# Output maps in fifteen even pieces, two features in every place, Gelu ahead of the map piece, and the weights' steps later in a turn

## The chip, the cores and the metric

The kernel runs on one core of one Trainium2 chip. The metric is the device time of one execution in microseconds (us). Three executions of the kernel before took 2920.89, 2920.94 and 2922.76 us, so its median is 2920.94 us.

## What is computed

The reference has two layers with a residual sum each. The first is a state-space layer: a kernel K of 2048 taps for each of 512 features, made from 64 complex modes, is convolved with the normalised input (8 rows of 2048 steps), Gelu follows, and the result is normalised and added. The second is a recurrent layer with gates f, i and g over 128 steps, of which only the last cell state is used, and an output product.

```
x = x + layernorm(gelu(conv(layernorm(x), K) + D * layernorm(x)))
for t in steps:
    c = sigmoid(xt @ wf.T + c @ uf.T + bf) * c + sigmoid(xt @ wi.T + c @ ui.T + bi) * tanh(xt @ wc.T + c @ uc.T + bc)
h = tanh(x @ wo.T + c_final @ uo.T + bo)
x = x + layernorm(h)
```

The shapes as the harness cuts them: x is 8 x 2048 x 512; the second layer goes over the first dimension, 8 steps of 2048 rows, so its eight blocks of 256 rows each run 8 steps.

## The kernel before

The work has three stages. A prologue (to about 141 us of the span) takes row statistics, makes K and the powers of the state matrix, and starts on the first group of features. The convolution stage (141.74 to 637 us) is where the change lies. The last stage, from there to the end, is the recurrent layer; the change does not touch it.

**The convolution stage.** The 512 features are cut into 16 groups of 32. The sequence is cut into 16 chunks of 128 steps. Within a chunk the convolution is a Toeplitz product (`conv_input`, float32, tiles `T` and `u`). Across chunks it goes through a state of 128 numbers: 15 states per group, each made from the one before (`state_in`, `state_high`, `state_low`), and an output map per feature, 128 x 128, applied to the states (`conv_state`, three float16 products per feature). The output map of a group is made by doubling: step k = -1 and 0 give single columns, step k doubles the number of columns from 2^k, and the last, k = 6, makes columns 64 to 127 (`outm`). Steps are cut into pieces by features, because a bank takes 512 columns: `PIECES` lists (k, first feature, last feature). There are 12 pieces in the kernel before, whose widths are 32, 32, 64, 128, 256 columns and then seven times 512.

A **turn** i (1 to 16) convolves group i-1 while it makes the states and the maps of group i. It has 16 **places** j. In place j stand state 15i+j (j below 15), piece j of the map (where there is one), the features that `CONV_AT[j]` names, and the weights' steps of that place. TensorE, ScalarE, VectorE and the queue of SyncE each run through the places in this order; every engine executes its own list strictly in the order in which it is written, and waits on semaphores.

- On TensorE a place is: `state_high(j)`, the two or so `conv_input`, `state_low(j)`, `state_in(j+1)`, the `conv_state`, then `outm(j)`, then `turn` or `spread` of the weights.
- State j goes from the bank through ScalarE (`state`, high half, L737) and VectorE (`state`, low half, L1001). `state_high(j+1)` waits for the first, `state_low(j+1)` (L1304) for the second.
- A map piece goes the same way: ScalarE L748, then VectorE L1011. The next step of the doubling waits for VectorE's part of the whole step before.
- A Gelu (L801) takes four features at once, so it stands in the places where the fourth feature of a bank is done.

**The weights.** In turns 1 to 15 the eight weight matrices of the second layer are split into float16 parts. A matrix set n goes through in turn n (n = 0 and 1 both in turn 1). For n mod 4 of 0 or 1 there are four maxima (`most`, VectorE L1069); for 1 there follow `most2` (VectorE L1071), `turn` (a transpose on TensorE, L1386), `most3` (VectorE L1074, L1075), `spread` (TensorE L1389) and `most4` (VectorE L1079 to L1082), which give the scale. For n mod 4 of 2 or 3 there are four `cut` (ScalarE L820) and four `cut2` (VectorE L1086), and then a store to `wd`. The places in which they stand are in `weight_steps`. Below, a turn with `cut` is a **cut turn** (2, 3, 6, 7, 10, 11, 14, 15) and one with `most` a **most turn** (1, 4, 5, 8, 9, 12, 13); of these 1, 5, 9 and 13 also have the five steps from `most2` to `most4`.

**Other engines.** GpSimd normalises `u` of group i+1 in turn i, with two instructions of 1024 columns for each of four quarters (L619, L621). The SyncE queue issues, at the start of turn i: four loads of `u` (which wait until the convolution of turn i-1 is done), the load of the weights `wts`, a load of `T` from `kpad`, the store of `y` of group i-2; later the second `T`, and in a cut turn the store of `wd` after `cut2` number 3. A DMA that has to wait for its semaphore holds everything behind it in this queue.

Of the kernel before, what the change touches and what calls it, by code (L numbers as in the profile page):

```python
# [16 lines left out]
G = 32  # L17
NG = H // G
# [62 lines left out]

def piece_done(g, k):

    return NP * g + max(i for i, p in enumerate(PIECES) if p[0] == k) + 1


def weight_steps(i):

    at = {j: [] for j in range(-1, 16)}

    def steps(n, places):
        if n % 4 < 2:
            names = [("load", 0)] + [("most", f) for f in range(4)]
            if n % 4:
                names += [("most2", 0), ("turn", 0), ("most3", 0), ("spread", 0), ("most4", 0)]
        else:
            names = [("load", 0)] + [("cut", f) for f in range(4)] + [("cut2", f) for f in range(4)]
        for j, (name, f) in zip(places, names):
            at[j].append((name, n, f))
# [6 lines left out]
    return at  # L106
# [49 lines left out]
def s4_lstm_program(nc, x, xr, xg, wts, cst, small, four, out):  # L156
    ctx = ExitStack()
    with ctx:
# [13 lines left out]
        s = {n: ctx.enter_context(nc.semaphore(f"s_{n}")) for n in names}  # L172
# [166 lines left out]
        def sync_program(e):  # L339
            w = Engine(e)  # L340
# [58 lines left out]
            for i in range(1, NG + 1):  # L399
                tasks = weight_steps(i)  # L400

                def weights(j):
                    for step, n, f in tasks[j]:
# [88 lines left out]
            for j in range(8):  # L492
                for b in range(8):
                    i = 8 * j + b
# [205 lines left out]
        def act_program(e):  # L700
# [38 lines left out]
            def outm(g, i):  # L739
                k, h0, h1 = PIECES[i]  # L740
                n = NP * g + i
# [61 lines left out]
            for i in range(1, NG + 1):  # L803
                tasks = weight_steps(i)
                for j in range(16):
                    if i < NG and j < 15:
                        state(15 * i + j)
                    if i < NG and j < NP:
                        outm(i, j)
                    for h in CONV_AT[j]:  # L810
                        conv(i - 1, h)
                    for step, n, f in tasks[j]:
# [69 lines left out]
        def dve_program(e):  # L882
# [120 lines left out]
            def outm(g, i):  # L1003
                k, h0, h1 = PIECES[i]
                n = NP * g + i
# [49 lines left out]
            for i in range(1, NG + 1):  # L1055
                tasks = weight_steps(i)
                for j in range(16):
# [4 lines left out]
                    for step, n, f in tasks[j]:  # L1062
# [145 lines left out]
        def pe_program(e):  # L1208
# [97 lines left out]
            def outm(g, i):  # L1306
                k, h0, h1 = PIECES[i]
                n = NP * g + i
# [27 lines left out]
            def conv_state(g, h):  # L1336
# [3 lines left out]
                w.wait_ge(s["omlo"], NP * g + NP)  # L1340
# [51 lines left out]
            for i in range(1, NG + 1):  # L1392
                tasks = weight_steps(i)
                for j in range(16):
# [14 lines left out]
                    for step, n, f in tasks[j]:  # L1409
                        weights(step, n)  # L1410
# [154 lines left out]
```

## Time and profile before

| | us |
|---|---|
| median of 3 runs | 2920.94 |
| the profiled execution, its own time | 2926.07 |
| its span, first to last instruction | 2924.3 |
| mean granted TensorE clock | 0.983 of full speed |
| TensorE busy / weight load busy | 2791.8 (95%) / 2285.4 (78%) |
| VectorE / ScalarE / GpSimd busy | 1664.1 (57%) / 994.7 (34%) / 790.0 (27%) |

All trace rows come from the profiled execution, which took 5.13 us longer than the median of the runs. 1.77 us of its time lie outside the span. Busy shares are means over three unlike stages; what the change can do has to be read in the convolution stage, turn by turn. A turn is counted here from the first `conv_input` of its place 0 to the first of the next turn. By that count turns 1 to 16 start at 141.74, 179.10, 210.77, 242.42, 276.11, 307.92, 339.47, 371.39, 402.71, 436.53, 468.19, 499.86, 531.27, 562.74, 594.25 and 623.59 us.

### The profile page before, as it was taken

To read this page: it belongs to the slowest core of one execution; us is meant where nothing else is said; L and a number is where in the kernel's file an instruction comes from. 1 tells how busy PE (TensorE), PEld (TensorE's weight loads), DVE (VectorE), ACT (ScalarE), POOL (GpSimd) and SP (SyncE) were. 2 spreads that over 40 slices of the span, in tenths; PEclk is the share of its full clock that TensorE was granted. 3 is DMA by queue.
4 is the path that set the end of the run, shared out by engine and by line. 5 is a ranking of instruction groups with operands and counts; after the bars stand their busy time and mean duration, and the time that the engine had idled before them with its cause. 6 is when DMAs were issued, how large, how long until landed. Compare 5 with 4: busy or idle time off the path is not lost.

```text
span 2924.3 us, 57067 instructions
## 1 busy us (share of the span) xinstructions
PE 2791.8 (95%) x23628; PEld 2285.4 (78%) x23628; DVE 1664.1 (57%) x3615; ACT 994.7 (34%) x1982; POOL 790.0 (27%) x1187
## 2 busy tenths in 40 slices
PE   3589999999999999999999999999999999999998
PEld 2377777778887788778877887788788878877884
DVE  7854545556456555665466556655655566456535
ACT  6655545542223322332223223222332232232223
POOL 7776656611112111221122112211221122112102
PEclk7799999999999999999999999999999999999999
DMA  8867768783222222222321322221322233222201
GB/s 322 282 226 256 244 219 279 251 288 94 48 46 61 66 64 50 65 63 60 71 66 45 81 43 70 69 59 37 80 65 52 44 77 69 47 52 71 66 14 58
DMA packets 404549, 308.65 MB, mean 106 GB/s; under 512 B 274368, under 2 KB 340416, under 8 KB 398016
## 3 DMA queue, kind: packets, MB, share of 16 engines
q1 hardware_dynamic: 404288, 305.00, 37.1%
q8 instruction: 185, 3.03, 0.4%
q14 instruction: 76, 0.62, 0.1%
HBM read 195.88 MB, written 76.02 MB: 93 GB/s over the span
## 4 chain that ended last, share of the span: by engine, by line
PE 86%; DVE 6%; DMA 4%; ACT 2%; issue 1%; SPq 1%; POOL 0%; DVEq 0%; POOLq 0%; ACTq 0%
PE bank L1433 34%; PE bank L1444 30%; PE bank L1472 10%; DMA big<-wts 3%; PE bank L1334 2%; PE bank L1284 2%; PE bank L1342 2%; PE bank L1320 2%; PE bank L1459 1%; DVE big L1086 1%; DVE big L1020 1%; PE bank L1296 1%; PE bank L1304 1%; DVE big L1011 1%; ACT big L748 1%
## 5 line engine op out<-in xcount | busy, mean ns | idle before, releaser
L1433 PE MATMUL bank<-big 128*128 128x256 f16 x9216 | 1038.7, 273 | 2.7 <-DVE big L1129 1.5
L1433 PEld LDWEIGHTS bank<-big 128*128 128x128 f16 x9216 | 902.4, 98 | 126.3 <-DVE big L1129 1.8
L1444 PE MATMUL bank<-big 128*128 128x256 f16 x8064 | 911.2, 273 | 0.0
L1444 PEld LDWEIGHTS bank<-big 128*128 128x128 f16 x8064 | 789.0, 98 | 95.8
L852 ACT ACTIVATE big<-bank,big 128x256 f32<-128x256 f32 x768 | 402.5, 561 | 1145.5 <-PE bank L1444 1128.6
L1158 DVE TENSOR_TENSOR big<-big 128x256 f32<-128x256 f32 x224 | 94.8, 423 | 574.2 <-ACT big L852 571.8
L1472 PE MATMUL bank<-big 128*128 128x512 f16 x1536 | 348.8, 379 | 0.0
L1472 PEld LDWEIGHTS bank<-big 128*128 128x128 f16 x1536 | 150.3, 98 | 160.3
L661 POOL TENSOR_SCALAR big<-big 128x1 f32<-128x1 f32 x128 | 33.0, 258 | 795.7 <-DVE big L1110 794.3
L676 POOL TENSOR_SCALAR big<-big 128x1 f32<-128x1 f32 x128 | 28.5, 223 | 796.3 <-DVE big L1189 796.3
L859 ACT ACTIVATE big<-big 128x512 f32<-128x512 f32 x128 | 80.6, 630 | 465.2 <-DVE big L1185 465.2
L1160 DVE TENSOR_TENSOR big<-big 128x256 f32<-128x256 f32 x256 | 108.9, 426 | 170.9 <-ACT big L852 164.6
L619 POOL TENSOR_TENSOR big<-big 128x1024 f32<-128x1024 f32 x63 | 150.8, 2394 | 155.5 <-DMA big<-xg 155.3
L1001 DVE SCALAR_TENSOR_TENSOR big<-bank,big 128x256 f16<-128x256 f32 x240 | 101.2, 422 | 122.7 <-ACT big L737 122.3
L1334 PE MATMUL bank<-big 128*128 128x128 f32 x1024 | 157.6, 279 | 1.5 <-POOL big L630 1.5
L621 POOL TENSOR_TENSOR big<-big 128x1024 f32<-128x1024 f32 x63 | 155.3, 2465 | 4.9
L1011 DVE SCALAR_TENSOR_TENSOR big<-bank,big 128x32 f16<-128x32 f32 (+2 forms) x192 | 101.7, 530 | 94.8 <-ACT big L748 94.3
L1284 PE MATMUL bank<-big 128*128 128x256 f32 x480 | 146.5, 388 | 6.4 <-DVE big L993 6.4
L1334 PEld LDWEIGHTS bank<-big 128*128 128x128 f32 x1024 | 134.4, 193 | 4.4 <-issue 1.9
L748 ACT ACTIVATE big<-bank 128x32 f16<-128x32 f32 (+2 forms) x192 | 91.1, 474 | 132.2 <-PE bank L1320 132.1
L1192 DVE TENSOR_TENSOR big<-big 128x512 f32<-128x512 f32 x128 | 88.7, 693 | 67.9 <-ACT big L866 67.1
L1342 PEld LDWEIGHTS bank<-big 128*128 128x128 f16 x1536 | 103.1, 98 | 30.9 <-issue 0.5
(188 smaller groups left out, 2865.2 us busy)
## 6 DMA issues: line engine op xcount, KB each, us to landing
big<-xr SPq DMA_DIRECT2D x16, 2048.0 KB, 11.1
big<-xg SPq DMA_DIRECT2D x64, 512.0 KB, 6.3
big<-kpad SPq DMA_DIRECT2D x32, 1024.0 KB, 11.7
yd<-big SPq DMA_DIRECT2D x16, 2048.0 KB, 17.3
big<-x SPq DMA_DIRECT2D x64, 512.0 KB, 6.0
out<-big SPq DMA_DIRECT2D x128, 256.0 KB, 2.1
big<-yd SPq DMA_DIRECT2D x62, 512.0 KB, 6.7
big<-wts SPq DMA_DIRECT2D x16, 1024.0 KB, 9.8
```

Source lines behind the costliest of these rows:

```text
L619: e.tensor_tensor(ug, ug, st(0), SUB).then_inc(s["sub"], 1)
L621: e.tensor_tensor(ug, ug, st(1), MUL).then_inc(s["nrm"], 1)
L748: e.activation(M[g % 2][:, 0, h0:h1, lo:lo + wide], o, ACT.Copy, scale=BACK).then_inc(s["omhi"], 1)
L852: e.activation(gt[m % 2][:, g, :], gate_out(m, g), ACT.Tanh if g == 2 else ACT.Sigmoid, bias=bs, scale=inv[g]).then_inc(s["ga"], 1)
L1011: e.scalar_tensor_tensor(Mg[:, 1, h0:h1, lo:lo + wide], o, BACK, Mg[:, 0, h0:h1, lo:lo + wide], MUL, SUB).then_inc(s["omlo"], 1)
L1160: ch().tensor_tensor(gb[:, 1, :], gb[:, 1, :], gb[:, 2, :], MUL).then_inc(s["c"], 1)
L1284: ins = e.matmul(o, Gm, u[g % 3][:, k].rearrange("p h b -> p (h b)"), start=True, stop=(k == 0))
L1334: e.matmul(o, T[t % 3][:, h % 16, :], u[g % 3][:, :, h, :], start=(q == 0), stop=False, skip_group_check=True)
L1342: ins = e.matmul(o[:, 1:16], M[g % 2][:, lw, h, :], X[g % 2][:, :, lx, h, :], start=False, stop=(a == 2), skip_group_check=True)
L1433: ins = e.matmul(gate_out(m, g), W[2 * g][:, lw, kt, m * 128:(m + 1) * 128], src[:, lx, kt, :], start=(n == 0 and g != 1), stop=last, skip ...
L1444: ins = e.matmul(gate_out(m, g), W[2 * g + 1][:, lw, kt, m * 128:(m + 1) * 128], src[:, lx, kt, :], start=False, stop=(n == 11), skip_grou ...
L1472: ins = e.matmul(bH[n % NH][:, :], x2T[i % R][:, lx, kt, cc * 128:(cc + 1) * 128], W[6][:, lw, kt, :], start=(a == 0), stop=(a == 11))
```

## The change

Four things change in the convolution stage, all of them in the order and the size of the work; no sum over columns changes.

1. **The maps.** Groups 1 to 15 get 15 pieces: the first six as before (32, 32, 64, 128, 256, 512 columns), step 5 in pieces of 12, 12 and 8 features (384, 384, 256 columns), step 6 in pieces of 6, 6, 5, 5, 5, 5 features (384, 384, 320, 320, 320, 320 columns). Group 0, made in the prologue, keeps the 12 pieces. `piece_base` counts the pieces for both.
2. **The features.** `CONVS` was 2 in places 0 to 10, 0 in place 11, 2 in 12 to 14 and 4 in 15; now it is 2 in each of the 16 places. Since a Gelu takes four features, it now stands in every odd place.
3. **ScalarE's order.** In a place the Gelu now stands ahead of the map piece.
4. **The weights' places.** `most` moves from places 4, 6, 8, 10 to 7, 8, 9, 10; `most2` and `turn` from 11 and 12 to 11 both; `most3` and `spread` from 13 and 14 to 12 both; `most4` from 15 to 13. `cut` moves from 5, 7, 9, 11 to 10, 11, 12, 13 and `cut2` from 6, 8, 10, 12 to 12, 13, 14, 15. In turn 1 the four `most` of n = 0 move from places 2, 2, 3, 3 to 7, 7, 8, 8; the load of n = 1 from place 4 to 8 and its `most` from 8, 8, 9, 9 to 14, 14, 15, 15; its five further steps from places 11 to 15 of turn 1 to places 0, 0, 1, 1, 2 of turn 2.

```diff
-PIECES = [(-1, 0, G)] + [(k, 0, G) for k in range(5)] + [(5, 0, 16), (5, 16, 32)] + [(6, 8 * i, 8 * i + 8) for i in range(4)]
+PIECES_0 = [(-1, 0, G)] + [(k, 0, G) for k in range(5)] + [(5, 0, 16), (5, 16, 32)] + [(6, 8 * i, 8 * i + 8) for i in range(4)]
+PIECES = PIECES_0[:6] + [(5, a, b) for a, b in ((0, 12), (12, 24), (24, 32))] + [(6, a, b) for a, b in ((0, 6), (6, 12), (12, 17), (17, 22), (22, 27), (27, 32))]
-CONVS = [2] * 11 + [0] + [2] * 3 + [4]
+CONVS = [2] * 16
...
+def piece_base(g):
+
+    return len(PIECES_0) + NP * (g - 1) if g else 0
...
-    if i == 1:
-        steps(0, (-1, 2, 2, 3, 3))
-        steps(1, (4, 8, 8, 9, 9, 11, 12, 13, 14, 15))
-    elif i < 16:
-        steps(i, (-1, 4, 6, 8, 10, 11, 12, 13, 14, 15) if i % 4 < 2 else (-1, 5, 7, 9, 11, 6, 8, 10, 12))
+        if n == 0:
+            at[1, -1].append(("load", n, 0))
+            places = [("most", f, 1, 7 + f // 2) for f in range(4)]
+        elif n == 1:
+            at[1, 8].append(("load", n, 0))
+            places = [("most", f, 1, 14 + f // 2) for f in range(4)]
+            places += [("most2", 0, 2, 0), ("turn", 0, 2, 0), ("most3", 0, 2, 1), ("spread", 0, 2, 1), ("most4", 0, 2, 2)]
         else:
+            at[n, -1].append(("load", n, 0))
+            if n % 4 < 2:
+                places = [("most", f, n, 7 + f) for f in range(4)]
+                if n % 4:
+                    places += [("most2", 0, n, 11), ("turn", 0, n, 11), ("most3", 0, n, 12), ("spread", 0, n, 12), ("most4", 0, n, 13)]
+            else:
+                places = [("cut", f, n, 10 + f) for f in range(4)] + [("cut2", f, n, 12 + f) for f in range(4)]
...
                 for j in range(16):
                     if i < NG and j < 15:
                         state(15 * i + j)
+                    for h in CONV_AT[j]:
+                        conv(i - 1, h)
                     if i < NG and j < NP:
                         outm(i, j)
-                    for h in CONV_AT[j]:
-                        conv(i - 1, h)
...
-                w.wait_ge(s["omlo"], NP * g + NP)
+                w.wait_ge(s["omlo"], piece_base(g + 1))
```

**Where the order moves.** TensorE in places 11 to 14 of turn 5. Before (L1320 is a map piece, L1296 and L1304 are `state_high` and `state_low`, L1334 `conv_input`, L1284 `state_in`, L1342 `conv_state`, L1386 `turn`, L1389 `spread`):

```order
L1320 MATMUL bank<-big 128x512 x3
L1296 MATMUL bank<-big 128x256 x2
L1334 MATMUL bank<-big 128x128 x2
L1304 MATMUL bank<-big 128x256
L1284 MATMUL bank<-big 128x256
L1342 MATMUL bank<-big 128x120 x6
L1386 MATMUL bank<-big 1x128
L1296 MATMUL bank<-big 128x256 x2
...
L1342 MATMUL bank<-big 128x120 x6
L1389 MATMUL bank<-big 128x1
```

The same engine and places now (L1332 is the map piece, L1398 `turn`, L1401 `spread`, L1308 and L1316 the state, L1346 `conv_input`, L1296 `state_in`, L1354 `conv_state`):

```order
L1354 MATMUL bank<-big 128x120 x6
L1332 MATMUL bank<-big 128x320 x3
L1398 MATMUL bank<-big 1x128
L1308 MATMUL bank<-big 128x256 x2
L1346 MATMUL bank<-big 128x128 x2
L1316 MATMUL bank<-big 128x256
L1296 MATMUL bank<-big 128x256
L1354 MATMUL bank<-big 128x120 x6
L1332 MATMUL bank<-big 128x320 x3
L1401 MATMUL bank<-big 128x1
```

`turn` stood behind a whole place of products after the last piece; now it stands directly behind the piece of its own place, and so does `spread`.

VectorE in places 6 to 8 of turn 2, a cut turn, before (L1001 is a state's low half, L1011 a map piece, L1086 `cut2`):

```order
L1011 SCALAR_TENSOR_TENSOR big<-bank,big 128x16x32
L1086 SCALAR_TENSOR_TENSOR big<-big 128x512
L1001 SCALAR_TENSOR_TENSOR big<-bank,big 128x256
L1011 SCALAR_TENSOR_TENSOR big<-bank,big 128x16x32
L1001 SCALAR_TENSOR_TENSOR big<-bank,big 128x256
L1011 SCALAR_TENSOR_TENSOR big<-bank,big 128x8x64
L1086 SCALAR_TENSOR_TENSOR big<-big 128x512
```

The same engine in places 12 to 15 of that turn and place 0 of the next, now (L1014 the state, L1024 the piece, L1098 `cut2`):

```order
L1024 SCALAR_TENSOR_TENSOR big<-bank,big 128x5x64
L1098 SCALAR_TENSOR_TENSOR big<-big 128x512
L1014 SCALAR_TENSOR_TENSOR big<-bank,big 128x256
L1024 SCALAR_TENSOR_TENSOR big<-bank,big 128x5x64
L1098 SCALAR_TENSOR_TENSOR big<-big 128x512
L1014 SCALAR_TENSOR_TENSOR big<-bank,big 128x256
L1024 SCALAR_TENSOR_TENSOR big<-bank,big 128x5x64
L1098 SCALAR_TENSOR_TENSOR big<-big 128x512 x2
L1014 SCALAR_TENSOR_TENSOR big<-bank,big 128x256
```

The four `cut2` stood in every second place from 6 on; now they stand one to a place at the end of the turn, the last two next to each other, ahead of the next turn's first state.

## Rows read from the trace of the kernel before

**Rows 1.** Windows: start:end, length, busy (instructions) of PE, PEld, DVE, ACT, POOL; clock, DMA

```profile
141.74:623.59 481.85, 449.34 (x4030) 361.51 (x4031) 245.61 (x496) 255.45 (x556) 284.81 (x118) 0.99 0.73 249
468.18:499.86 31.68, 29.53 (x272) 23.77 (x270) 17.60 (x31) 18.15 (x39) 19.68 (x8) 1.00 0.78 266
594.25:623.59 29.34, 29.27 (x270) 23.24 (x267) 15.13 (x31) 18.04 (x39) 0.00 (x0) 1.00 0.92 319
```

**Rows 2.** TensorE's waits from 142 to 630 us: who waited for whom, total, times, longest

```profile
PE bank L1304 <- DVE big L1001: 29.4, 35, 3.7
```

**Rows 3.** Timeline, two most turns: start, us, engine, line [idle before <-releaser]

```profile
244.80 0.33 SPq L409 DMA_DIRECT2D big<-wts  x1
255.04 0.69 DVE L1069 TENSOR_REDUCE big<-big 128x1 f32<-128x512 f32 x1 [3.32 <-DMA big<-wts]
256.12 0.28 PE L1304 MATMUL bank<-big 128*128 128x256 f16 x1 [2.43 <-DVE big L1001]
512.93 0.28 PE L1304 MATMUL bank<-big 128*128 128x256 f16 x1 [1.81 <-DVE big L1001]
```

**Rows 4.** Groups of lines by form, 140 to 640 us: xcount | busy, mean ns | idle before

```profile
L801 ACT ACTIVATE big<-bank,big 128x512 f32<-128x512 f32 x128 | 87.6, 685 | 34.1 <-PE bank L1342 34.1
L748 ACT ACTIVATE big<-bank 128x512 f16<-128x512 f32 x105 | 62.7, 597 | 88.2 <-PE bank L1320 88.0
L748 ACT ACTIVATE big<-bank 128x256 f16<-128x256 f32 x15 | 5.8, 384 | 11.1 <-PE bank L1320 11.1
L1011 DVE SCALAR_TENSOR_TENSOR big<-bank,big 128x512 f16<-128x512 f32 x105 | 72.2, 688 | 62.5 <-ACT big L748 62.1
L1011 DVE SCALAR_TENSOR_TENSOR big<-bank,big 128x256 f16<-128x256 f32 x15 | 6.4, 425 | 9.9 <-ACT big L748 9.9
L1069 DVE TENSOR_REDUCE big<-big 128x1 f32<-128x512 f32 x32 | 21.8, 680 | 20.3 <-DMA big<-wts 20.2
```

**Rows 5.** Window after the wait at 256.12, columns as in rows 1

```profile
256.70:260.20 3.50, 3.50 (x18) 2.55 (x17) 1.25 (x3) 0.72 (x2) 3.42 (x2) 0.51 1.04 439
```

**Rows 6.** Timeline of a cut turn, places 6 and 10

```profile
481.79 2.40 POOL L619 TENSOR_TENSOR big<-big 128x1024 f32<-128x1024 f32 x1
482.30 2.44 DVE L1086 SCALAR_TENSOR_TENSOR big<-big 128x512 f16<-128x512 f32 x1
485.13 0.28 PE L1304 MATMUL bank<-big 128*128 128x256 f16 x1 [1.18 <-DVE big L1001]
493.23 0.74 DVE L1086 SCALAR_TENSOR_TENSOR big<-big 128x512 f16<-128x512 f32 x1
```

**Rows 7.** Timeline: start of place 5 in turn 4; two places of a cut turn

```profile
250.69 0.38 PE L1296 MATMUL bank<-big 128*128 128x256 f16 x2
...
486.65 0.38 PE L1296 MATMUL bank<-big 128*128 128x256 f16 x2
...
488.82 0.38 PE L1296 MATMUL bank<-big 128*128 128x256 f16 x2
...
489.02 0.60 ACT L748 ACTIVATE big<-bank 128x512 f16<-128x512 f32 x1 [1.01 <-PE bank L1320]
```

**Rows 8.** Timeline: SyncE's queue and what follows it, turns 12 and 15

```profile
500.06 1.76 SPq L354 DMA_DIRECT2D big<-xg  x4
503.75 2.40 POOL L619 TENSOR_TENSOR big<-big 128x1024 f32<-128x1024 f32 x1 [11.61 <-DMA big<-xg]
620.52 0.32 SPq L413 DMA_DIRECT2D wd<-big  x1
637.55 0.96 DVE L1099 COPY big<-big 128x64 f32<-128x64 f32 x4 [13.39 <-ACT big L801]
```

**Rows 9.** Timeline of turn 13: the steps for the scale

```profile
557.14 0.15 DVE L1071 TENSOR_REDUCE big<-big 128x1 f32<-128x8 f32 x1
559.40 0.27 DVE L1074 TENSOR_REDUCE big<-bank 1x1 f32<-1x128 f32 x1
559.70 0.14 DVE L1075 TENSOR_SCALAR big<-big 1x1 f32<-1x1 f32 x1
```

More of the change, by code:

```diff
@@ L79, in norm_place, with pieces, weight_places @@
     return n if n < 3 else n - 1
+def pieces(g):
+    return PIECES if g else PIECES_0
+def piece_base(g):
+    return len(PIECES_0) + NP * (g - 1) if g else 0
 def piece_done(g, k):
[L84 to L95, printed above, removed]
-        else:
-            names = [("load", 0)] + [("cut", f) for f in range(4)] + [("cut2", f) for f in range(4)]
-        for j, (name, f) in zip(places, names):
-            at[j].append((name, n, f))
-    if i == 1:
-        steps(0, (-1, 2, 2, 3, 3))
-        steps(1, (4, 8, 8, 9, 9, 11, 12, 13, 14, 15))
-    elif i < 16:
-        steps(i, (-1, 4, 6, 8, 10, 11, 12, 13, 14, 15) if i % 4 < 2 else (-1, 5, 7, 9, 11, 6, 8, 10, 12))
+    return piece_base(g) + max(i for i, p in enumerate(pieces(g)) if p[0] == k) + 1
+def weight_places():
+    at = {(i, j): [] for i in range(1, NG + 1) for j in range(-1, 16)}
+    for n in range(NG):
+        if n == 0:
[5 more added lines that the diff above has]
+            places += [("most2", 0, 2, 0), ("turn", 0, 2, 0), ("most3", 0, 2, 1), ("spread", 0, 2, 1), ("most4", 0, 2, 2)]
+        else:
+            at[n, -1].append(("load", n, 0))
[5 more added lines that the diff above has]
+                places = [("cut", f, n, 10 + f) for f in range(4)] + [("cut2", f, n, 12 + f) for f in range(4)]
+        for step, f, i, j in places:
+            at[i, j].append((step, n, f))
     return at
+WEIGHTS_AT = weight_places()
 def win_used(n):
@@ L399, in sync_program @@
             for i in range(1, NG + 1):
-                tasks = weight_steps(i)
                 def weights(j):
-                    for step, n, f in tasks[j]:
+                    for step, n, f in WEIGHTS_AT[i, j]:
                         m = 2 * (n // 4) + n % 2
@@ L739, in outm @@
             def outm(g, i):
-                k, h0, h1 = PIECES[i]
-                n = NP * g + i
+                k, h0, h1 = pieces(g)[i]
+                n = piece_base(g) + i
                 wide = 1 if k < 0 else 2 ** k
@@ L803, in act_program @@
             for i in range(1, NG + 1):
-                tasks = weight_steps(i)
                 for j in range(16):
@@ L807, in act_program @@
                         state(15 * i + j)
+                    for h in CONV_AT[j]:
+                        conv(i - 1, h)
                     if i < NG and j < NP:
                         outm(i, j)
-                    for h in CONV_AT[j]:
-                        conv(i - 1, h)
-                    for step, n, f in tasks[j]:
+                    for step, n, f in WEIGHTS_AT[i, j]:
                         if step == "cut":
@@ L1003, in outm @@
             def outm(g, i):
-                k, h0, h1 = PIECES[i]
-                n = NP * g + i
+                k, h0, h1 = pieces(g)[i]
+                n = piece_base(g) + i
                 wide = 1 if k < 0 else 2 ** k
@@ L1061, in dve_program @@
                         outm(i, j)
-                    for step, n, f in tasks[j]:
+                    for step, n, f in WEIGHTS_AT[i, j]:
                         g = n // 4
@@ L1306, in outm @@
             def outm(g, i):
-                k, h0, h1 = PIECES[i]
-                n = NP * g + i
+                k, h0, h1 = pieces(g)[i]
+                n = piece_base(g) + i
                 Mg = M[g % 2]
@@ L1408, in pe_program @@
                         outm(i, j)
-                    for step, n, f in tasks[j]:
+                    for step, n, f in WEIGHTS_AT[i, j]:
                         weights(step, n)
```

2 lines of the change are left out of this document (removed).

## The prediction, made before the changed kernel was run

> **What bounds the kernel now.** I read the page first, then the convolution stage alone: its turns as windows, TensorE's waits, and the timeline around each wait. The windows [rows 1] show that turns 1 to 15 take 481.85 us, with TensorE busy for 449.34, so TensorE bounds them. ScalarE and VectorE are busy for about half, so they matter only by when they deliver. The same rows show one turn that hardly waits: turn 15, 29.34 us, against 31.68 for turn 10 with the same products. A reader should ask what the others spend 2 to 8 us on.
>
> The list of waits names one relation, `state_low` waiting for VectorE's low half of the state, 29.4 us in 35 waits [rows 2]. VectorE is late for two reasons.
>
> First, the maxima. VectorE stands at the first `most` until the weights have landed, 10.24 us after their issue (255.04 - 244.80), and the state queued behind it is late: TensorE stops for 2.43 us [rows 3]. These waits for DMA are 20.2 us in total [rows 4], in seven turns. After 2.43 us the clock also fell to 1.2 GHz: granted 0.51 over the next 3.5 us [rows 5], which costs some 1.7 us. After a stop of 1.81 us, the last of these rows [rows 3], it did not.
>
> Second, `cut2`. At 482.30 it takes 2.44 us while GpSimd runs its L619 from 481.79 to 484.19; at 493.23, with GpSimd done, it takes 0.74 [rows 6]. It seems to begin only as GpSimd's instruction ends. That holds up the state behind it and gives TensorE's stop of 1.18 us. Turn 15, in which GpSimd is idle [rows 1], has no such stop.
>
> The Trainium skill, "SBUF — State Buffer", section "SBUF: two separate sides", says that VectorE with two SBUF inputs and GpSimd take a shared port pair as an exclusive lock for a whole instruction. `cut2` has two such inputs, and 2.44 against 0.74 agrees. By that rule the move pays only if GpSimd is done by place 12.
>
> **The change, part by part.** Base of a turn: turn 15's 29.34, less about 0.4 in its place 10 where ScalarE does a map piece, a Gelu and a `cut` in a row ahead of a state (an estimate), is 28.95.
>
> *Even pieces and two features everywhere.* The columns stay. A full place takes 488.82 - 486.65 = 2.17 us [rows 7]; of this three products of 512 columns are 0.64 us at 2.4 GHz. New full places take 2.0 (384 columns) or 1.93 (320). Nine more products a turn cost what their start costs; the bounds are 0 and 0.05 us each, I take 0.005, so 0.05 a turn, inside the base. On ScalarE a piece of 512 takes 597 ns, of 256 384; on VectorE 688 and 425 [rows 4]. From the slope a piece of 0 columns would be 0.17 and 0.16 us, so three more pieces are 0.5 us on each engine and turn, under idle time.
>
> *Gelu ahead of the piece.* The bank of the features is ready about 0.45 us before that of the piece (320 or 384 columns), so most of the Gelu (685 ns [rows 4]) runs while TensorE makes the piece. Before, ScalarE's row in such a place was piece, Gelu, `cut`, state: 0.60 + 0.69 + 0.72 before the state. Now piece and `cut` alone follow the moment at which TensorE ends the place: 0.44 + 0.72, and the state's bank is ready 1.1 us into the next place. So that delay goes. The price is that the piece starts up to 0.2 us later; the next level of doubling needs it more than a place's 1.5 us of other products later, so it is covered.
>
> *`cut2` in places 12 to 15.* GpSimd starts 3.7 us after the first load (503.75 - 500.06 [rows 8]) and is busy for 19.7 us of a turn [rows 1], so it ends 23.4 us into the turn. Place 5 begins 8.27 us into a turn (250.69 [rows 7] - 242.42, turn 4's start), and place 12 so 22.3 us in (8.27, then 2.17, 2.0, 2.0, 1.85, 2.0, 2.0 and 1.93 for places 5 to 11), its `cut2` after the piece at about 25.3. So four `cut2` of 0.74 each: 1.23 us in a place with state 0.42 and piece 0.49 is 1.65, under 1.93. The last two follow each other; the next turn's first state comes through about 1.7 us into that turn, and `state_low` of place 1 asks at 2.0. Cut turns then take the base.
>
> *The store behind it.* In SyncE's queue the store of `wd` now waits for the last `cut2`, some 1.3 us after the turn's end, and the four loads of `u` stand behind it. Its 1 MB also goes first. In turns 3, 7 and 11, cut turns behind cut turns, GpSimd so starts up to 4 us later and ends at 25 to 27, beside the first `cut2` at 25.3. That costs VectorE up to 1.7 us, of which 0.6 is slack. Bounds 0 and 1.7 a turn; I take 1.1, as the stop of 1.18 at place 8's state is the nearest row [rows 6]: 3.3 us.
>
> The Trainium skill, "DMA: Bandwidth & Descriptors", section "Queues, rings and completion order", says that each DMA engine consumes one issuer's descriptors in ring order. By it the full megabyte delays the loads. No row here has the two next to each other.
>
> *`most` in places 7 to 10.* Place 7 starts 12.5 us in and reaches its `most` at about 16. The weights are issued 2.4 us in (4 behind a store) and land 10.2 later, so the wait is gone in all turns. A maximum (680 ns [rows 4]) in four places in a row leaves 0.2 us of delay: 6 turns, 1.2 us. In turn 1 two stand in place 7: 0.8, and ScalarE's table load of about 1.2 stays: 2.0.
>
> *The scale.* This part costs. `turn` stands directly behind the piece of its own place, but `most2` stands on VectorE behind its part of that piece. From TensorE's last product: 0.20 to ScalarE (489.02 against 488.82 [rows 7]), or 0.37 where a Gelu still runs, the piece 0.44, VectorE's part 0.49 (both from the slope above), `most2` 0.15 [rows 9]: 1.45, with hand-overs 1.5 us in which TensorE stands. `spread` waits likewise: 0.20 + 0.44 + 0.49, then L1074 and L1075, 0.44 with their gap [rows 9]: 1.6. With 0.4 for the two products themselves 3.5 us in turns 5, 9 and 13: 10.5. In turn 2 they stand in places 0 and 1, behind the maxima of n = 1, which end 2.3 us into it: 1.8 + 1.8 + 0.4 = 4.0.
>
> *Sum.* 15 x 28.95 = 434.3; turn 1 2.0; turn 2 4.0; turns 5, 9, 13 10.5; maxima 1.2; late GpSimd 3.3: together 455.3 against 481.85, so 26.6 us less. Two clock drops seen here (turns 4 and 9) and that of turn 1 are out of it by working up from the base.
>
> *The hand-over to the last stage.* The store of turn 15 was issued at 620.52, 3.1 us before turn 16 [rows 8]; now it comes 1.4 after its start, and the loads of x and y, which were issued 0.2 to 1.3 us into turn 16, stand behind it and a load of 1 MB. VectorE's copies at 637.55 came when the Gelu was done, not by DMA [rows 8]. The bounds are 0 and 4.5 us (620.52 to 625.0); since the copies wait 13.4 us for the Gelu, part of it is room, and I take 1.6.
>
> So 25.0 us less: the profiled execution would take 2901.1, and from the median of the runs 2920.94 - 25.0 = 2895.9 us. I forecast 2896.
>
> **Rivals.**
>
> *A. The scale's waits bring the clock down.* Four pairs of stops of 1.5 to 1.8 us, with one place between them. For it: a stop of 2.43 brought it down [rows 3, 5]. Against: 1.81 did not. One drop each costs 1.7, two 3.5: 7 to 14 us more, about 2906.
>
> *B. The store holds up more than I took.* The weights of turns 4, 8 and 12 are issued 4 us in and land after 16, so `most` waits again; with 2 us and a drop each (3.7) plus the upper bound in turns 3, 7, 11 (1.8) and at the hand-over (2.9): 16 us more, about 2912. For it: DMA is busy for 0.78 of a cut turn [rows 1].
>
> *C. Slower: the Gelu ahead of the piece.* In places 1, 3, 5, 7 and 9 the Gelu begins before the piece's bank is ready, so the piece's high half comes about 0.4 us later than it would alone. In places 1 and 3 the next level needs VectorE's part 1.5 us after the next place begins, and I find only 0.25 us of room there. If the Gelu holds the piece for 1 us more than its 0.69 (an access to the bank, or a change of function such as the one table load in turn 1), TensorE stops for 0.7 us in five places of 15 turns, 52 us, and the time is about 2948; it becomes slower from 0.33 us a place. Against: the waits of TensorE name only the state, not the piece [rows 2], and ScalarE is busy for 18.15 of 31.68 us [rows 1].
>
> *D. The waits move.* VectorE's and ScalarE's steps are the same number; if the state is late behind four `cut2` as it was behind two, the seven cut turns with GpSimd keep 31.5 instead of 28.95: 18 us of the gain go, 2914. Against: the stop follows GpSimd's instruction [rows 6], and turn 15 does not show it.
>
> **Chances.** Forecast 0.55, with a range of its own of 2889 to 2902; A 0.16; B 0.11; D 0.08; C and slower 0.05; the rest, 0.05, ends below 2889, if neither store nor hand-over costs anything. A range of 2887 to 2912 takes in the forecast, A and about half of B. This kernel can be told from no change at about 0.2%, 5.8 us. Faster 0.88, no change 0.06, slower 0.06.
>
> **What would show it.** In the changed profile: no wait for DMA ahead of the maxima, and granted clock 1.00 in turns 4 and 9; `cut2` at 0.74 us in turns 2, 6, 10, 14, and one longer one each in 3, 7, 11; cut turns of about 29, most turns 4, 8, 12 of 29.2, and 5, 9, 13 of 32.5, slower than before in two of three; TensorE waiting at L1398 and L1401 for VectorE, 1.5 us each. It would be wrong if L1316 still waited for 1 us in cut turns, or if clock 0.5 stood behind L1398.

## The result, and the profile after

| | before | after |
|---|---|---|
| median of 4 runs, us | 2920.91 | 2899.2 |
| lowest to highest | 2916.88 to 2922.76 | 2898.09 to 2899.8 |
| profiled execution, its own time / its span | 2926.07 / 2924.3 | 2899.8 / 2898.0 |

The ratio is 0.9927, with a 95% interval of 0.991 to 0.9944. So the changed kernel is 21.7 us faster; the forecast was 25.0 us less, 2896.

The windows of the kernel after, columns as in [rows 1], answer to [rows 1]: turns 1 to 15 together, then turn 5 (with the scale), turn 6 (a cut turn behind a most turn), turn 11 (a cut turn behind a cut turn), turn 15, and 3.3 us behind the wait of `turn` in turn 5:

```profile
140.44:594.18 453.74, 438.18 (x4166) 372.63 (x4166) 237.72 (x539) 266.39 (x601) 280.53 (x118) 1.00 0.78 262
263.99:296.32 32.33, 29.63 (x284) 24.91 (x281) 15.86 (x41) 16.66 (x38) 19.04 (x8) 1.00 0.67 228
296.32:325.20 28.88, 28.88 (x281) 24.72 (x278) 14.14 (x34) 18.66 (x42) 19.05 (x8) 1.00 0.77 255
445.49:475.65 30.16, 29.04 (x281) 24.69 (x278) 17.13 (x36) 18.77 (x42) 19.05 (x8) 1.00 0.82 280
565.74:594.18 28.44, 28.44 (x280) 24.41 (x276) 14.96 (x35) 18.66 (x42) 0.00 (x0) 1.00 0.95 332
288.10:291.40 3.30, 1.89 (x19) 1.36 (x17) 1.24 (x4) 0.82 (x2) 0.00 (x0) 1.00 0.02 5
```

Turns 1 to 15 take 453.74 us where they took 481.85. In turn 6 TensorE is busy for the whole 28.88, so nothing is left to wait for there. All fifteen, in order: 31.58, 32.89, 30.21, 28.87, 32.33, 28.88, 30.21, 28.87, 32.34, 28.87, 30.16, 28.88, 32.33, 28.88, 28.44.

The three largest of TensorE's waits from 142 to 610 us, which answer to [rows 2]:

```profile
PE bank L1398 <- DVE big L1083: 5.7, 4, 1.9
PE bank L1401 <- DVE big L1087: 5.7, 4, 1.4
PE bank L1316 <- DVE big L1014: 3.8, 4, 1.2
```

`state_low` (L1316 here) waits 4 times for 3.8 us, not 35 times for 29.4. New are `turn` (L1398) and `spread` (L1401), 11.4 us together. The groups by form, 140 to 610 us, which answer to [rows 4]:

```profile
L1098 DVE SCALAR_TENSOR_TENSOR big<-big 128x512 f16<-128x512 f32 x32 | 28.2, 902 | 0.0
L1081 DVE TENSOR_REDUCE big<-big 128x1 f32<-128x512 f32 x32 | 21.7, 677 | 0.2
```

The maxima (L1081) have 0.2 us of idle time ahead of them where they had 20.3, and none for DMA. The mean of `cut2` (L1098), 902 ns over 32, hides two kinds: 0.74 for nearly all, and 2.41 to 2.46 for the first one of turns 3, 7 and 11.

Three places of the timeline (start, us, engine, line, idle before and its releaser): a cut turn behind a cut turn, the scale of turn 5, and GpSimd's start in turn 11. They answer to [rows 3], [rows 6] and [rows 9].

```profile
229.75 2.39 POOL L635 TENSOR_TENSOR big<-big 128x1024 f32<-128x1024 f32 x1
...
230.25 2.45 DVE L1098 SCALAR_TENSOR_TENSOR big<-big 128x512 f16<-128x512 f32 x1
...
233.08 0.28 PE L1316 MATMUL bank<-big 128*128 128x256 f16 x1 [1.16 <-DVE big L1014]
...
285.91 0.57 PE L1332 MATMUL bank<-big 128*128 128x320 f16 x3
287.77 0.27 PE L1398 MATMUL bank<-big 128*1 128x128 f32 x1 [1.29 <-DVE big L1083]
...
291.38 0.38 PE L1401 MATMUL bank<-big 1*128 1x1 f32 x2 [1.41 <-DVE big L1087]
...
453.31 2.39 POOL L633 TENSOR_TENSOR big<-big 128x1024 f32<-128x1024 f32 x1 [13.26 <-DMA big<-xg]
```

GpSimd begins 7.8 us into turn 11 (453.31 - 445.49), and 7.8 to 7.9 into turns 3 and 7. Its last instruction of turn 3 still runs at the first `cut2`, which takes 2.45 us instead of 0.74, and TensorE's state stops for 1.16.

The hand-over, on SyncE, VectorE and TensorE (turn 16 starts at 594.18), answers to [rows 8]:

```profile
596.04 0.32 SPq L427 DMA_DIRECT2D wd<-big  x1
596.40 0.43 SPq L387 DMA_DIRECT2D big<-wd  x1
596.88 2.03 SPq L455 DMA_DIRECT2D big<-x  x2
599.01 8.24 SPq L464 DMA_DIRECT2D big<-yd  x2
...
610.06 0.42 DVE L1111 COPY big<-big 128x64 f32<-128x64 f32 x2 [13.82 <-DMA big<-yd]
611.84 0.42 DVE L1111 COPY big<-big 128x64 f32<-128x64 f32 x2 [1.36 <-DMA big<-yd]
...
616.07 1.44 PE L1494 MATMUL bank<-big 128*128 128x1 f16 x48 [5.17 <-DMA big<-wd]
...
623.17 1.23 PE L1444 MATMUL bank<-big 128*128 128x256 f16 x5 [1.46 <-DVE big L1141]
```

The copies before took their release from the Gelu; now it comes from the load of y, 1.36 us apart. From the start of turn 16 to the first product of the gates (623.17) it is 28.99 us, before 25.82 (649.41 - 623.59): 3.2 us given back. From that product to the last instruction both need the same (2274.89 and 2274.83).

The two profiles so differ by 26.3 us of span: 28.1 in the turns, 1.3 in an earlier start of the stage, less 3.2 at the hand-over. The earlier start is not the change's: the profiles of all kernels here, whose prologues do the same work, begin this stage between 140.44 and 142.64 us, that of `weights_only` last. Without it the profiles differ by 24.9 us, and the medians of the runs by only 21.7. Why, the first experiment shows in part.

### The profile page after: what moved, and what is told of

It is laid out like the page before. It is cut to its first block, busy times and chain, and to the rows that moved or that the text cites. A ratio compares the mean times of both kernels' runs of the same rounds, so it can differ in the third digit from the quotient of the medians.

```text
span 2898.0 us, 57427 instructions
## 1 busy us (share of the span) xinstructions
PE 2780.0 (96%) x23763; PEld 2295.7 (79%) x23763; DVE 1656.5 (57%) x3660; ACT 1005.7 (35%) x2027; POOL 785.8 (27%) x1187
## 4 chain that ended last, share of the span: by engine, by line
PE 92%; DVE 4%; ACT 1%; issue 1%; DMA 1%; POOL 0%; SPq 0%; POOLq 0%; DVEq 0%; ACTq 0%
PE bank L1444 35%; PE bank L1455 30%; PE bank L1483 10%; PE bank L1346 4%; PE bank L1296 3%; PE bank L1332 3%; PE bank L1354 3%; PE bank L1308 2%; PE bank L1470 1%; PE bank L1316 1%; DVE big L1033 1%; ACT big L879 0%; DMA big<-yd 0%; DVE big L1197 0%; DMA big<-xr 0%
## 5 line engine op out<-in xcount | busy, mean ns | idle before, releaser
L1024 DVE SCALAR_TENSOR_TENSOR big<-bank,big 128x320 f16<-128x320 f32 (+6 forms) x237 | 108.9, 460 | 155.1 <-ACT big L762 154.9
L1346 PE MATMUL bank<-big 128*128 128x128 f32 x1024 | 158.3, 277 | 1.5 <-POOL big L644 1.5
L1296 PE MATMUL bank<-big 128*128 128x256 f32 x480 | 145.7, 386 | 6.4 <-DVE big L1006 6.4
L1346 PEld LDWEIGHTS bank<-big 128*128 128x128 f32 x1024 | 135.2, 192 | 5.0 <-issue 1.9
L1014 DVE SCALAR_TENSOR_TENSOR big<-bank,big 128x256 f16<-128x256 f32 x240 | 101.0, 421 | 63.1 <-ACT big L751 58.7
L1354 PEld LDWEIGHTS bank<-big 128*128 128x128 f16 x1536 | 104.2, 98 | 33.0 <-issue 0.3
L1332 PE MATMUL bank<-big 128*128 128x320 f16 (+6 forms) x711 | 126.3, 287 | 1.4 <-DVE big L1024 1.3
```

Of the source, the lines that this page charges most:

```text
L1024: e.scalar_tensor_tensor(Mg[:, 1, h0:h1, lo:lo + wide], o, BACK, Mg[:, 0, h0:h1, lo:lo + wide], MUL, SUB).then_inc(s["omlo"], 1)
L1296: ins = e.matmul(o, Gm, u[g % 3][:, k].rearrange("p h b -> p (h b)"), start=True, stop=(k == 0))
L1332: ins = e.matmul(o, Ak[:, max(k, 0), lw, :], r, start=(a == 0), stop=(a == 2))
L1346: e.matmul(o, T[t % 3][:, h % 16, :], u[g % 3][:, :, h, :], start=(q == 0), stop=False, skip_group_check=True)
L1354: ins = e.matmul(o[:, 1:16], M[g % 2][:, lw, h, :], X[g % 2][:, :, lx, h, :], start=False, stop=(a == 2), skip_group_check=True)
```

## The experiments

The theory after the result: the gain comes from the weights' places, by two mechanisms (`most` no longer waits for its DMA, `cut2` no longer meets GpSimd); the pieces and the Gelu's place bring little; the two waits of the scale, the store ahead of the loads of `u`, and the late last store each give something back. The rival theory: the even pieces or the Gelu's place bring the gain, and the waits went with them.

The experiments' runs come from three series. The median of the kernel before was 2920.65, 2921.12 and 2919.92 us in them, so a difference between medians of different series is uncertain by about 1 us.

**1. The kernel before once more** (no edit), one execution, profiled.

> The kernel before once more, for a second profile. The first profile took 2926.07 us, 5.2 above the median of its runs (2920.91). Theory: each turn in which the maxima wait for the weights' DMA may or may not bring TensorE to 1.2 GHz, 1.7 us each; this profile shows one to three windows at 0.5 in the convolution stage, and its time is 2917 to 2926 by their number. Rival: the difference lies elsewhere (prologue or last stage); then the turns take 481.9 us again and the rest differs.

Measured: 2921.98 us, near its median. Windows: 3.5 us behind the stop of 2.81 us in turn 5, and turns 1 to 15:

```profile
286.90:290.40 3.50, 3.50 (x20) 2.34 (x20) 0.79 (x2) 0.98 (x2) 3.42 (x2) 0.63 1.07 425
141.98:619.53 477.55, 447.27 (x4031) 360.15 (x4031) 246.92 (x496) 255.64 (x556) 284.16 (x118) 0.99 0.74 251
```

The turns take 477.55 us here, 4.3 less than in the profile from which the forecast was made. The pattern of stops is the same, but their lengths differ from run to run: in most turns 1, 4, 5, 8, 9, 12 and 13 they were 2.59, 1.24, 2.81, 0.94, 1.55, 1.18 and 1.24 us, and the clock fell only behind the first and the third. In the first profile it fell in turns 1, 4 and 9. The seven stops were 14.6 us together in the first profile and are 11.6 here, so of the 4.3 us the shorter stops are 3.1, and one clock drop fewer covers the rest. Against this execution the change gains 23.8 us in the turns (477.55 - 453.74) and gives back 3.2: 20.6, where the runs show 21.7. Of the 23.8 us, 13.2 lie in the eight cut turns, 6.0 in the most turns 4 to 13 and 4.6 in turn 1; no run moves the maxima alone. With the stage's start, 1.5 us earlier in the profile of after, it is 22.2, the difference of the spans (2920.2 - 2898.0).

**2 and 3. The weights' places alone, and the rest alone.** `weights_only` has the new places with the old pieces, the old features and the Gelu behind the piece:

```diff
-PIECES = PIECES_0[:6] + [(5, a, b) for ...] + [(6, a, b) for ...]
+PIECES = PIECES_0
-CONVS = [2] * 16
+CONVS = [2] * 11 + [0] + [2] * 3 + [4]
-                    for h in CONV_AT[j]:
-                        conv(i - 1, h)
                     if i < NG and j < NP:
                         outm(i, j)
+                    for h in CONV_AT[j]:
+                        conv(i - 1, h)
```

> The kernel before with only the weights' steps moved (old 12 pieces, old features per place, Gelu behind the piece). Theory: the gain comes from two things alone, the maxima no longer wait for DMA and cut2 no longer meets GpSimd; so cut turns take 29 to 29.4 us, turns 4, 8 and 12 about 29.2, and the time is 2899 to 2904. Rival: even pieces and the Gelu's place carry at least half; then it stays at 2908 or above.

Measured: 2900.71 us (2899.52 to 2902.58), ratio 0.9928 [0.9911, 0.9944]. `order_only` has the new pieces, features and Gelu with the weights in their old places:

```diff
+    steps(1, 0, (-1, 2, 2, 3, 3))
+    steps(1, 1, (4, 8, 8, 9, 9, 11, 12, 13, 14, 15))
+    for i in range(2, 16):
+        steps(i, i, (-1, 4, 6, 8, 10, 11, 12, 13, 14, 15) if i % 4 < 2 else (-1, 5, 7, 9, 11, 6, 8, 10, 12))
```

> The changed kernel with the weights' steps in their old places (even pieces, two features per place, Gelu ahead). Theory: the waits for DMA at the first maximum stay at 1.3 to 2.4 us and cut2 still takes 1.8 to 2.4 us twice a cut turn; only the shorter queue of ScalarE helps: 2913 to 2919. Rival (pieces and Gelu carry half): below 2910.

Measured: 2912.65 us (2911.06 to 2915.48), ratio 0.9971 [0.9959, 0.9982], just below what was expected. TensorE's largest waits from 142 to 610 us with the new places alone, then from 142 to 620 us without them (L1313 is `state_low`):

```profile
PE bank L1398 <- DVE big L1083: 5.2, 4, 1.5
PE bank L1401 <- DVE big L1087: 2.6, 4, 1.0
PE bank L1308 <- ACT big L751: 2.3, 9, 1.0
```

```profile
PE bank L1313 <- DVE big L1011: 24.4, 21, 2.8
```

The places alone give 20 of the 21.7 us and take all of `state_low`'s waits away; without them 24.4 us of these waits stay. The two halves do not add up (20 + 8 is more than 21.7). A likely reason, which no run isolates: both shorten the same stops, and what one has taken away the other cannot take again. Pieces, features and the Gelu's place together bring 8 us with the weights in the old places, but only 1.5 on top of the new ones. Two features in every place were not run by themselves.

**4. GpSimd idle.** The kernel before, with GpSimd's two instructions cut to one block of 128 x 8 from group 3 on, so `u` is not normalised there; its waits, signals and all loads stay.

```diff
+                if n >= 12:
+                    ug = u[g % 3][:, 4 * q, 0:1, :]
+                    st = lambda r: mvk[:, 4 * q, :, r].unsqueeze(1)
```

> The kernel before, in which GpSimd normalises only a single chunk column block of each quarter from group 3 on (so the values of u stay unnormalised there); all waits and DMAs are the same. Theory (cut2 waits for GpSimd's running instruction): every cut2 takes 0.74 us, the stop of 1.2 us at place 8 is gone, cut turns from 2 on take 29.3 to 29.8 us instead of 31.6: about 12 us less, 2907 to 2911. Rival (cut2 is late because ScalarE and VectorE are crowded): cut2 keeps 1.8 to 2.4 us, 2919 to 2922.

Measured: 2907.19 us (2906.88 to 2910.71), ratio 0.9952 [0.9937, 0.9967]. Groups by form, 250 to 600 us, where L1089 is `cut2`:

```profile
L1089 DVE SCALAR_TENSOR_TENSOR big<-big 128x512 f16<-128x512 f32 x23 | 17.1, 743 | 0.0
L624 POOL TENSOR_TENSOR big<-big 128x8 f32<-128x8 f32 x40 | 8.1, 202 | 3.1
```

All 23 take 0.74 us, in their old places, and so do the nine before the window. So `cut2` is long because GpSimd works beside it, and not because of where it stands; the cut turns with GpSimd fall from between 31.5 and 31.9 us to between 29.8 and 30.7. The trace also shows how it is held up. In the profiles of before and after 17 `cut2` start beside a GpSimd instruction; they take 1.60 to 2.46 us, and each of them ends 0.55 us behind that instruction's end (482.30 + 2.44 against 481.79 + 2.40 in [rows 6]). So `cut2` is not slowed down by a factor: it stands until GpSimd's instruction is over. The median is 13.5 us below that of before in the same series (2920.65), by a change of the work of another engine alone.

**5. The Gelu behind the piece.** After, with only this edit undone:

```diff
-                    for h in CONV_AT[j]:
-                        conv(i - 1, h)
                     if i < NG and j < NP:
                         outm(i, j)
+                    for h in CONV_AT[j]:
+                        conv(i - 1, h)
```

> The changed kernel with ScalarE's Gelu behind the map piece again. Theory: only in places 11 and 13 of the eight cut turns, where piece, Gelu and cut stand in a row, does the state come late; 0.3 to 0.7 us a cut turn, so 2901 to 2905. Rival C of the prediction (the Gelu ahead holds up the piece and costs): then it is faster than the changed kernel, below 2897.

Measured: 2900.22 us (2898.56 to 2901.7), ratio 0.9929 [0.9914, 0.9944] to before, below the 2901 to 2905 expected. Turns 6, 8, 10 and 14 of 28.88 us take 29.11 here, but 4 and 12 are the same and 5, 9 and 13 are 0.17 us shorter (32.16). Over turns 2 to 15 the two profiles differ by 0.3 us, and by 0.8 for the Gelu ahead if turn 7 is left aside, in which the first `cut2` met only the last 0.03 us of a GpSimd instruction here and took 0.74. The runs, 1.0 us apart, cannot tell the edit from nothing. ScalarE in turn 6 of after shows why rival C did not come true:

```profile
306.31 0.69 ACT L815 ACTIVATE big<-bank,big 128x512 f32<-128x512 f32 x1 [0.36 <-PE bank L1354]
306.96 0.60 ACT L762 ACTIVATE big<-bank 128x512 f16<-128x512 f32 x1
```

The piece (L762) begins 0.65 us after the Gelu, as its duration allows, and takes the same 0.60 us as before [rows 4].

**6. The old pieces.** After, with `PIECES = PIECES_0`.

> The changed kernel with the old 12 map pieces (seven of 512 columns, places 5 to 11) for all groups; features, Gelu and weights' places as changed. Theory: TensorE has the same columns, so turns without a stop take 28.8 to 29.2 us; the places 12 to 14 without a piece are only 1.5 us long and hold a cut and a cut2 each, so a little of the state's delay comes back: 2899 to 2904. Rival (even pieces carry a gain of their own by a shorter chain): above 2906.

Measured: 2898.99 us (2898.29 to 2900.07), ratio 0.9925 [0.991, 0.994]: the same as after. TensorE's waits, 142 to 600 us:

```profile
PE bank L1398 <- DVE big L1083: 5.8, 4, 1.5
PE bank L1401 <- DVE big L1087: 3.0, 4, 1.4
PE bank L1316 <- DVE big L1014: 0.8, 3, 0.3
```

The cut turns 3, 6, 7, 10, 11 and 14 take 29.27 to 29.78 us instead of 28.87 to 30.21, turns 5, 9 and 13 take 31.83 instead of 32.33. The pieces save 0.4 us in a cut turn that meets nothing, and lose it again elsewhere: with twelve pieces place 12 has none, so `spread` waits 0.55 us in turns 5, 9 and 13 instead of 1.41, and in turns 3, 7 and 11 the stop at the state is 0.33 us at most instead of 1.16.

**7. `turn` and `spread` one place behind the steps they need.**

```diff
-            places += [("most2", 0, 2, 0), ("turn", 0, 2, 0), ("most3", 0, 2, 1), ("spread", 0, 2, 1), ("most4", 0, 2, 2)]
+            places += [("most2", 0, 2, 0), ("turn", 0, 2, 1), ("most3", 0, 2, 2), ("spread", 0, 2, 3), ("most4", 0, 2, 4)]
-                    places += [("most2", 0, n, 11), ("turn", 0, n, 11), ("most3", 0, n, 12), ("spread", 0, n, 12), ("most4", 0, n, 13)]
+                    places += [("most2", 0, n, 11), ("turn", 0, n, 12), ("most3", 0, n, 13), ("spread", 0, n, 14), ("most4", 0, n, 15)]
```

> The changed kernel with turn and spread one place behind the maximum that they wait for (most2 11, turn 12, most3 13, spread 14, most4 15; for n = 1 in places 0 to 4 of turn 2). Theory: the eight stops at L1398 and L1401 (11.4 us in the trace, 13 with the hand-overs) go: turns 5, 9 and 13 take 29.3 us instead of 32.3 and turn 2 29.5 instead of 32.9, time 2885 to 2889. Rival: the state waits in their place (VectorE has the same work in the same turn): 2893 or above.

Measured: 2888.8 us (2887.36 to 2890.42), ratio 0.989 [0.9874, 0.9907]; 10.4 us below after. All its waits of TensorE from 142 to 600 us:

```profile
PE bank L1316 <- DVE big L1014: 5.2, 5, 1.5
PE bank L1494 <- ACT big L815: 0.8, 1, 0.8
PE bank L1332 <- DVE big L1024: 0.6, 1, 0.6
```

L1398 and L1401 are gone from the list. Turns 5, 9 and 13 take 29.65 us instead of 32.33: 2.7 each. Turn 2 gains 2.4, not the 3.3 of its two stops (1.85 and 1.42), since a stop of 0.96 at a state comes in.

**8. The cuts of turn 15 earlier.** `cut` in places 8 to 11 and `cut2` in 9 to 12, in turn 15 alone, where GpSimd has nothing to do.

```diff
-                places = [("cut", f, n, 10 + f) for f in range(4)] + [("cut2", f, n, 12 + f) for f in range(4)]
+                c0 = 8 if n == NG - 1 else 10
+                places = [("cut", f, n, c0 + f) for f in range(4)] + [("cut2", f, n, (c0 + 1 if n == NG - 1 else 12) + f) for f in range(4)]
```

> The changed kernel with the cuts of turn 15 in places 8 to 11 and its cut2 in places 9 to 12 (GpSimd is idle there), so that the last store of wd is issued before turn 16 begins. Theory: the 3.2 us that the hand-over to the last stage takes longer than before (from turn 16's start to L1444) come back, since the copies wait for y's DMA behind this store: 2895 to 2897. Rival: the hand-over is bound by the DMA's total bytes whatever the order: 2899.

Measured: 2897.02 us (2896.1 to 2897.88), ratio 0.9918 [0.9903, 0.9933]. The timeline of its hand-over (turn 16 starts at 595.11):

```profile
592.82 0.32 SPq L428 DMA_DIRECT2D wd<-big  x1
...
609.17 0.95 DVE L1112 COPY big<-big 128x64 f32<-128x64 f32 x4 [13.38 <-ACT big L816]
```

The store is issued 2.3 us ahead of turn 16, the copies are released by the Gelu again, and the first product of the gates comes 25.91 us into turn 16 instead of 28.99. The profile shows 3.1 us; the medians differ by 2.2, their two ranges of runs do not overlap, but the intervals of the ratios do.

**9. The store behind the loads.** In the cut turns but the last, SyncE issues the store of `wd` behind the loads of `u`, the weights and `T` of the next turn.

```diff
-                        if step == "cut2" and f == 3:
+                        if step == "cut2" and f == 3 and n == NG - 1:
...
+                if 3 <= i < NG and (i - 1) % 4 >= 2:
+                    m = 2 * ((i - 1) // 4) + (i - 1) % 2
+                    w.wait_ge(s["w_hi"], 4 * (m + 1))
+                    w.wait_ge(s["w_lo"], 4 * (m + 1))
+                    e.dma_start(wd[m].rearrange("p l k o -> p l (k o)"), wout).then_inc(s["wd"], 16)
```

> The changed kernel with the store of wd of the turns 2, 3, 6, 7, 10, 11 and 14 issued at the start of the next turn behind the loads of u, wts and T instead of ahead of them. Theory (the store holds up the loads of u, so GpSimd in turns 3, 7 and 11 still works when the first cut2 comes): the cut2 of 2.4 us and TensorE's stop of 1.15 us in these three turns go, 30.2 us become 28.9: 4 us less, 2894 to 2897. Rival: the collision comes from the length of the turn, not from the order in the queue: unchanged, 2898 to 2900.

Measured: 2894.91 us (2894.72 to 2896.97), ratio 0.9916 [0.9902, 0.9931]; 4.3 us below after, or 3.3 when each is taken against the kernel before of its own series. The ranges of runs do not overlap, but the intervals of the ratios do. Turn 3 as a window, then its `cut2` on the timeline:

```profile
204.02:232.90 28.88, 28.88 (x282) 24.71 (x278) 15.42 (x36) 18.66 (x42) 18.97 (x8) 1.00 0.84 292
```

```profile
229.36 0.74 DVE L1103 SCALAR_TENSOR_TENSOR big<-big 128x512 f16<-128x512 f32 x1
```

Turns 3, 7 and 11 take 28.87 to 28.88 us instead of 30.16 to 30.21, and the first `cut2` 0.74 instead of 2.45. So the store ahead of the loads was what made GpSimd late. The edit takes away two things at once, the queue's wait for the last `cut2` and the megabyte; rows of after tell them apart. Turn 10 (from 416.62) has no store ahead of its loads, turn 11 (from 445.49) has one:

```profile
416.81 1.76 SPq L370 DMA_DIRECT2D big<-xg  x4
...
420.71 2.39 POOL L633 TENSOR_TENSOR big<-big 128x1024 f32<-128x1024 f32 x1 [13.10 <-DMA big<-xg]
...
446.92 0.32 SPq L427 DMA_DIRECT2D wd<-big  x1
447.28 3.10 SPq L370 DMA_DIRECT2D big<-xg  x4
```

The loads are issued 1.79 us into turn 11 instead of 0.19: 1.6 us are the wait in the queue. From that issue GpSimd begins 6.03 us later (453.31) instead of 3.90: the other 2.1 us are the megabyte ahead.

**10. The three edits of 7, 8 and 9 together.**

> The changed kernel with all three edits: turn and spread one place apart from their maxima, the last cuts in places 8 to 12 of turn 15, and the stores of wd behind the loads. Theory: they touch different turns, so they add: 10.4 (apart) + 2.2 (early_last) + 4 (store_later) less than 2899.2, so 2881 to 2885. Rival: TensorE's clock or the last stage takes part of it back: 2886 to 2890.

Measured: 2881.79 us (2881.38 to 2882.13), ratio 0.987 [0.9854, 0.9887]; 17.4 us below after, where the three alone gave 10.4, 2.2 and 4.3, together 16.9 (against the kernel before of each series: 16.4, and 16.3 for the sum). Turns 1 to 15, and TensorE's waits from 142 to 600 us:

```profile
140.89:578.82 437.93, 435.76 (x4165) 371.75 (x4166) 234.37 (x541) 265.64 (x601) 279.99 (x118) 1.00 0.80 272
```

```profile
PE bank L1322 <- DVE big L1020: 1.3, 2, 1.0
PE bank L1500 <- DMA big<-wd: 0.9, 1, 0.9
PE bank L1500 <- ACT big L821: 0.8, 1, 0.8
PE bank L1338 <- DVE big L1030: 0.6, 1, 0.6
```

TensorE is idle for 2.2 of 437.93 us there, so in these turns there is hardly anything left to win by order alone.

## Why the prediction was right, and by how much its terms were off

The forecast, 2896 us, was 3.2 us too low. The mechanisms were as told, but errors of single terms cancelled; here are the steps, each against the trace of after.

- **Base of a turn**: 28.95 forecast; 28.87 or 28.88 in the turns 4, 6, 8, 10, 12 and 14. Over 15 turns 1.2 us too much, and turn 15 is 0.4 shorter still. The pieces and the Gelu's place, which were to carry this term, are in it with 0.4 and 0.2 us in a cut turn without a stop (experiments 6 and 5), not more: with the weights' places alone such a turn already takes 29.70 us instead of 31.7.
- **`most` in places 7 to 10**: no DMA wait is left, as forecast. Turns 4, 8 and 12 take the bare base of 28.87, so the 1.2 us for the maxima were not needed.
- **`cut2` behind GpSimd**: right. Turns 6, 10 and 14 have no stop, and experiment 4 shows the cause from the other side. The exclusive lock that the Trainium skill describes ("SBUF — State Buffer", section "SBUF: two separate sides") agrees with this case: the only thing taken away was GpSimd's work, and `cut2` fell to 0.74 us in every place; and beside GpSimd it ended 0.55 us behind GpSimd's instruction, whatever it took. The forecast put the first `cut2` at 25.3 us into the turn, and it came at 25.33. (The starts of its places add up to 22.2 and not 22.3, and its 3.7 us for GpSimd run from the first load, 0.2 after the turn's start; neither mattered.)
- **Late GpSimd in turns 3, 7 and 11**: forecast 1.1 us each, measured 1.3 (30.21 - 28.88). GpSimd began 7.8 us into the turn, as the forecast's 3.7 and up to 4 more had it; experiment 9 shows that the store is the cause, by 1.6 us of waiting in the queue and 2.1 of its bytes. The collision takes 1.7 us of VectorE (2.45 against 0.74), of which 0.4 are slack.
- **The scale**: forecast 3.5 us in turns 5, 9, 13 and 4.0 in turn 2; measured 32.33 - 28.87 = 3.5, and 32.89 - 28.87 = 4.0. The stops are 1.29 and 1.41 us (forecast 1.5 and 1.6). Experiment 7 confirms it: without them it is 10.4 us faster, on top of the 21.7 that the change gains. **Rival A** fell: behind stops of 1.29 to 1.85 us the granted clock is 1.00.
- **Turn 1**: forecast 30.95, measured 31.58, of which about 1.4 us is a clock drop at its start (below); `apart` and `store_later`, with the same turn 1 and without the drop, take 30.19. So its own part is 1.3 and not 2.0.
- **The hand-over**: this term was mis-sized, 1.6 forecast and 3.2 measured, within the bounds of 0 to 4.5. I took most of the copies' 13.4 us of waiting as room, but that room was needed: the load of y was issued 4.8 us into turn 16 (599.01 - 594.18) and landed after the Gelu. Experiment 8 takes 3.1 of it back (28.99 - 25.91) by issuing the store 4.2 us earlier.
- **The difference taken from one profile**: the error that is left over. The sum of the turns was 455.3 forecast against 453.74 measured (1.4 of it the clock drop of turn 1), so the new turns were if anything better than forecast; but the old ones were read from an execution that took 5.1 us more than the median. The forecast subtracted the new turns from the old ones, 26.6 us, and then took that off the median of the runs. In the profiles its 25.0 us met 24.9 (28.1 - 3.2), because 1.6 us too little gain in the turns and 1.6 us too little loss at the hand-over cancelled, by luck; the whole miss of 3.2 comes from reading the gain in single executions, above all in that one of before. From the execution of experiment 1, which lies 1.1 us from the median, the same sum would have given 477.55 - 455.3 = 22.3 and with the forecast's hand-over 20.7, 2900. How many drops and how long stops the median run has, no run shows: of runs without a trace the mean clock is on record to 0.001 alone, which is 2.9 us, and it is 0.983 for the run of 2925.2 us but 0.984 for that of 2926.46.

**Rival B** had one half right, the store's mechanism in turns 3, 7, 11 and at the hand-over; its other half, that the maxima of turns 4, 8 and 12 wait again, did not come. In turn 4 the weights were issued at 240.35, 5.2 us into it, and the first maximum at 250.92 did not wait. **Rival C** fell by experiment 5 and **rival D** by turns 6, 10 and 14.

## What to carry to other kernels

Where a step of one engine is short, ask which place its own queue has reached when its data and its neighbours are ready; here moving at most nine small steps a turn gave 20 us, and resizing the large ones on top of that nothing that the runs can tell. Put a step that answers another engine's small step at least one block of work behind it, even when the small step is 0.15 us: what stands ahead of it in the other queue counts, not itself. And when a forecast is a difference to one profiled execution, first bring that execution to the median: compare its stops and clock drops with those of a second one, or the gain contains them.

## What was not expected of the hardware

- A longer stop did not always bring the clock down, and a shorter one did. Windows of 3.5 us, columns as in [rows 1]: the kernel before, behind its stop of 2.00 us in turn 9; then `order_only`, behind its stops of 2.75 us in turn 1 and 2.07 in turn 12:

```profile
416.60:420.10 3.50, 3.50 (x19) 2.43 (x18) 1.83 (x4) 1.06 (x3) 3.42 (x2) 0.58 1.01 427
```

```profile
152.40:155.90 3.50, 3.50 (x35) 2.93 (x34) 1.99 (x5) 2.05 (x5) 3.42 (x3) 1.00 1.26 307
499.90:503.40 3.50, 3.50 (x35) 2.92 (x34) 1.91 (x4) 2.00 (x5) 3.42 (x3) 1.00 1.05 432
```

- The clock also fell where the stage begins, in the profiles of after, `early_last`, `old_pieces` and `gpsimd_idle` (granted 0.51 to 0.73 from 141 to 143 us), and not in the other eight, with the same wait of 1.49 or 1.50 us ahead; among these `apart`, `store_later` and `best` have the same first instructions of the stage as after. First after, then `apart`:

```profile
141.00:143.00 2.00, 2.00 (x16) 1.58 (x15) 0.00 (x0) 0.31 (x1) 1.92 (x2) 0.51 1.02 383
```

```profile
141.00:143.00 2.00, 2.00 (x22) 1.83 (x23) 0.20 (x1) 0.31 (x1) 2.00 (x1) 1.00 0.97 371
```

What decides in either case stays open; no run here was made for it. The twelve profiles have eight stops of 2.00 to 3.72 us in turns 1 to 15; behind six of them the clock fell, behind the two of `order_only` it did not. Turns 4, 5 and 9 of the two profiles of before differ by 1.3 to 1.7 us more than their stops do, which is the price of such a drop. So in a sum it is a chance and not a fixed term.

- The length of a wait for DMA varies from run to run in the same place: TensorE's stop in turn 5 of the kernel before was 1.65 us in the first profile and 2.81 in experiment 1. With it goes the drop (34.3 us for the turn against 31.81), so one execution of this kernel can differ from the next by several us, as its runs from 2915.68 to 2926.46 do. The runs of `best`, which has no such waits, lie within 0.8 us.
- A store of 1 MB ahead of four loads in one queue, waiting for its own data first, made GpSimd's start 7.8 us into a turn instead of 4.1 (420.71 - 416.62 in turn 10), nearly twice as late.
